# A fused perceiver layer on one core: two counted loops on the engines written out as straight code

## The chip, the core and the metric

The kernel runs on one core of a Trainium2 chip. It has five instruction streams: TensorE (PE, whose weight loads the profile shows apart as PEld), VectorE (DVE), ScalarE (ACT), GpSimd (POOL) and SyncE (SP, which here only issues DMAs). Each works through its own program, and they meet only at semaphores. The metric is device time in microseconds; lower is better.

## What is computed

64 sequences of 32 tokens, 256 features each, in float32 (2048 tokens). The reference, cut to what matters:

```python
def layer(x, ctx_1024, ...):
    # 1: cross attention over 257 context rows per sequence, keys through a cosine
    K_hat = cos((ctx @ Wk + bk) @ Wr + br)
    x = x + softmax((layernorm(x) @ Wq + bq) @ K_hat.T) @ (ctx @ Wv + bv)
    # 2: self attention over the 8 most similar earlier tokens, then a gated gelu
    h = layernorm(x); A = causal_topk(h @ h.T / 16, 8)
    msg = softmax(where(A, (h @ Wq2.T) @ (h @ Wk2.T).T / sqrt(32), -1e9)) @ h
    x = x + gelu((mix * h + (1 - mix) * msg) * gain + bias) * scale
    # 3: mixture of 8 experts, one per token
    e = argmax(layernorm(x) @ Wr); p = max(softmax(layernorm(x) @ Wr))
    return x + p * (gelu(layernorm(x) @ W1[e] + b1[e]) @ W2[e] + b2[e])
```

## The kernel before

**Groups and steps.** The 2048 tokens are 16 groups (`NG`) of 128. A function `step` exists on PE, DVE, ACT and POOL; step s works on group s in stage 0 (`now`: transposing the context rows, projecting them, the cosine), on group s-1 in stage 1 (`one`: softmax and weighted sum), s-2 in stage 2 (`two`: similarities, the 8 best), s-3 in stage 3 (`three`) and s-4 in stage 4 (`four`: gelu, router). So there are 21 steps, s = 0 to 20, and from step 4 to step 15 all five stages are at work. From step 7 on, odd steps also do the ranks of the router for a pair of groups (`rank`, `places`, `scatter`). The order of instructions on each engine is written out by hand in `step`, and semaphore waits stand before the instructions that need them.

**Expert blocks.** Tokens sorted by expert are run in 23 blocks (`NBLK`) of 128 rows. Each block gathers its rows (`gather`, POOL L445), transposes them (`in_T`, PE L1255 into pK), multiplies by the expert's W1 (`up`, PE L1334: 32 matmuls), takes the gelu (ACT L1154), multiplies by W2 (`down`, PE L1348: 16 matmuls), adds and stores (`result`, DVE L862, `store`, POOL L451). Blocks 0 to 6 (`EARLY` = 7) are mixed into steps 16 to 20 and a short straight piece behind them. Blocks 7 to 22 are `late_block`s.

**What is a loop.** `run_steps` writes steps 0 to 5 out (`PEELED` = 6), then runs a counted loop on each engine of two turns of four steps (steps 6 to 9 and 10 to 13), then writes steps 14 to 20 out. SP has a loop of its own over the same groups (L593). `run_late` runs blocks 7 to 18 as a loop of three turns of four blocks on PE, DVE and ACT and writes blocks 19 to 22 out; POOL and SP have the late blocks written out already. In a loop the group number is a register, so the count that a semaphore has to reach is a register too:

```python
def at_least(eng, sem, count):
    if not isinstance(count, int) or count > 0:
        eng.wait_ge(sem, count)

def settle(eng, sem):
    eng.wait_ge(sem, 1)

def in_register(eng, count):
    return count if isinstance(count, int) else eng.to_reg(count)
```

`settle` is a wait that is always met, placed ahead of waits on registers.

**The names in the rows.** `stage` holds context rows, their transposes and the cosine's inputs and outputs; `pT` and `pK` are the PSUM banks of the context transposes and projections, and of the expert blocks later. The first DVE instruction of a step is the copy `stage<-pT` (L739, `ctx_T_copy`), the first on PE are eight transposes into `pT` (L1255), then two of `xn`, then the scores (L1407).

Of the kernel before, what the change touches and what calls it, by code (L numbers as in the profile page):

```python
# [45 lines left out]
PEELED = 6  # L46

def at_least(eng, sem, count):

    if not isinstance(count, int) or count > 0:
# [12 lines left out]

def upto(value, most):

    return min(value, most) if isinstance(value, int) else value

def groups(k, parity, behind):

    g = 2 * k + parity - behind
    if isinstance(g, int) and not 0 <= g < NG:
        return None
    return g, (parity - behind) % 2, k + (parity - behind) // 2

def pair(k, kp):  # L80

    q = k - 3
    if isinstance(q, int) and not 0 <= q < NG // 2:
        return None
    return q, 2 * ((kp + 1) % 2)

def run_steps(eng, step):

    for s in range(PEELED):  # L90
        step(s // 2, s % 2, s // 4, s // 2 % 2)
    with eng.Fori(0, (NG - 2 - PEELED) // 4) as i:
        for k, half, kp in ((3 + 2 * i, 1 + i, 1), (4 + 2 * i, 2 + i, 0)):
            step(k, 0, half, kp)
            step(k, 1, half, kp)
    for s in range(NG - 2, NG + STAGES):
        step(s // 2, s % 2, s // 4, s // 2 % 2)

def run_late(eng, block):  # L100

    turns = WAVES[-1][1] // SLOTS
    with eng.Fori(0, turns - 1) as k:
        for q in range(SLOTS):
            block(EARLY + SLOTS * k + q, (EARLY + q) % SLOTS, k + (EARLY + q) // SLOTS)
    for q in range(SLOTS):
        j = EARLY + SLOTS * (turns - 1) + q
        block(j, j % SLOTS, j // SLOTS)

def following(j, q, turn):
    return j + 1, (q + 1) % SLOTS, turn + (q + 1) // SLOTS

def perceiver_layer(nc, a, out):
    ctx = ExitStack()
    with ctx:
# [221 lines left out]
        def _(pool):  # L339
# [72 lines left out]
            def scatter(q, r0, turn):  # L412

                s = r0 // 2
                count = in_register(pool, 16 + 32 * turn)
                settle(pool, S["consts"])
                pool.wait_ge(tokens_st[s], count)
                pool.tensor_copy(token_now[:, r0:r0 + 2], token_all[:, bass.ds(2 * q, 2)]).then_inc(S["token_r"], 1)
                count = in_register(pool, q + 1)
                settle(pool, S["consts"])  # L420
# [7 lines left out]
            def count_pair(q):  # L428
                count = in_register(pool, q + 1)
                settle(pool, S["consts"])  # L430
                pool.wait_ge(S["onehot_r"], count)
                pool.tensor_copy(so_far[:, 0, :], so_far[:, 2, :]).then_inc(S["count_r"], 1)
                settle(pool, S["consts"])
# [21 lines left out]
            def step(k, parity, half, kp):  # L455
                now, one, two, three, four, coming = (groups(k, parity, n) for n in (0, 1, 2, 3, 4, -1))
                routed, s = pair(k, kp), 2 * k + parity if isinstance(k, int) else None
# [4 lines left out]
                if now:  # L462
                    g, b, _ = now
                    if isinstance(g, int) and g == 0:
                        pool.wait_ge(S["khat_last_r"], 1)

                    settle(pool, S["consts"])
# [7 lines left out]
                if two:  # L475
                    g, b, _ = two
                    count = in_register(pool, g - 1)
                    settle(pool, S["consts"])
# [4 lines left out]
                if one:  # L483
                    g, b, q = one

                    counts = [in_register(pool, n) for n in (g + 1, 16 * BG * (q + 1))]
                    settle(pool, S["consts"])
# [39 lines left out]
            run_steps(pool, step)  # L527
# [11 lines left out]
        def _(sp):  # L539
# [49 lines left out]
            for g in range(2, PEELED):  # L589
# [986 lines left out]
```

## Time and profile before

| | |
|---|---|
| median of 3 timed runs | 520.58 us (519.25, 520.58, 527.82) |
| the profiled execution, its own time | 522.69 us |
| its span (first to last instruction) | 520.6 us |
| PE busy / DVE busy / ACT busy / POOL busy | 456.7 / 286.1 / 268.8 / 186.8 us |
| mean granted TensorE clock | 0.948 of full speed |

The span is what the trace covers; 2.1 us of the profiled execution lie around it. "Busy" counts only instructions that an engine's datapath executes. Waits, register arithmetic, branches and the issue of DMAs don't count.

### The profile page before, as it was taken

The numbers are of one execution on the slowest core, as the hardware profiler recorded it, in microseconds if no ns is written. First come the engines' busy times: TensorE is split into PE (matmuls) and PEld (weight loads), VectorE is DVE, ScalarE is ACT, GpSimd is POOL, SyncE is SP. The second block draws the span as 40 slices with busy tenths as digits, with TensorE's granted clock in tenths as the row PEclk, the third lists the DMA queues.
The fourth block names the chain that finished last, engine by engine and source line by source line (L and its number), as shares of the span: only waits on it lengthen the run. The fifth ranks groups of instructions, "written<-read, shape, count | busy, mean of one in ns | idle before, by whom it ended". The sixth has DMA issues, their size and how long they took to land. (4 is left out here: it accounts for less than half of the span.)

```text
span 520.6 us, 10379 instructions
## 1 busy us (share of the span) xinstructions
PE 456.7 (88%) x2839; PEld 336.9 (65%) x2840; DVE 286.1 (55%) x904; ACT 268.8 (52%) x587; POOL 186.8 (36%) x326
## 2 busy tenths in 40 slices
PE   4889999999999759999999167985977999999992
PEld 3545565666666426666665055885967899999992
DVE  1556778888898548898898334763321121222220
ACT  2366768877788527788777233534213132233320
POOL 2732235334653414653545043442231332223210
PEclk9799999999999969999999768899999899999997
DMA  8612522325415305415551090353549556555300
GB/s 229 206 39 93 171 92 64 110 93 173 132 44 171 91 1 171 132 43 170 171 174 42 0 362 22 99 207 118 146 124 373 150 203 212 206 178 171 125 0 1
DMA packets 49106, 69.13 MB, mean 133 GB/s; under 512 B 8702, under 2 KB 38976, under 8 KB 48932
## 3 DMA queue, kind: packets, MB, share of 16 engines
q1 hardware_dynamic: 42820, 59.12, 34.6%
q0 software_dynamic: 3520, 8.23, 4.6%
q10 hardware_dynamic: 2720, 1.26, 0.9%
q8 instruction: 18, 0.29, 0.2%
q14 instruction: 28, 0.23, 0.2%
HBM read 62.20 MB, written 7.30 MB: 133 GB/s over the span
## 5 line engine op out<-in xcount | busy, mean ns | idle before, releaser
L1311 PE MATMUL pK<-stage,Wkr 128*128 128x512 f32 x256 | 126.2, 619 | 9.8 <-DVE stage L739 9.2
L1154 ACT ACTIVATE XF<-pT,b_now 128x128 f32<-128x128 f32 x184 | 52.6, 368 | 119.3 <-PE pT L1334 82.3
L1334 PE MATMUL pT<-XF,stage 128*128 128x128 f32 x736 | 92.0, 285 | 4.5 <-DMA stage<-in_L_ffn_W_dram 4.5
L1334 PEld LDWEIGHTS pT<-XF,stage 128*128 128x128 f32 x736 | 90.9, 201 | 6.9 <-issue 5.8
L1348 PE MATMUL pK<-W,XF 128*128 x368 | 87.0, 387 | 2.9 <-issue 1.3
L1348 PEld LDWEIGHTS pK<-W,XF 128*128 128x128 f32 x368 | 68.7, 193 | 12.6 <-issue 3.9
L1311 PEld LDWEIGHTS pK<-stage,Wkr 128*128 128x128 f32 x256 | 45.3, 196 | 48.7 <-issue 48.2
L356 POOL TENSOR_SCALAR ve<-mv 128x1 f32<-128x1 f32 x48 | 13.3, 276 | 157.2 <-DVE mv L662 157.1
L1135 ACT ACTIVATE stage<-pK,bkr 128x512 f32<-128x512 f32 x64 | 42.9, 689 | 34.5 <-PE pK L1311 33.0
L1142 ACT ACTIVATE stage<-stage 128x512 f32<-128x512 f32 x64 | 40.5, 633 | 20.4 <-DVE stage L734 20.2
L734 DVE TENSOR_TENSOR stage<-stage 128x512 f32<-128x512 f32 x64 | 47.7, 746 | 1.2
L445 POOL DMA_INDIRECT f_row<-rows_by_token,token_i x23 | 22.7, 987 | 71.1 <-DMA out_dram<-XF,token_i 37.7
L451 POOL DMA_INDIRECT out_dram<-XF,token_i x23 | 23.4, 1017 | 65.1 <-DVE XF L862 62.8
L1255 PE MATMUL pT<-ident,stage 128*128 128x128 f32 x260 | 36.4, 284 | 7.3 <-DMA br<-in_L_xattn_br_dram 6.5
L855 DVE COPY XF<-pK 128x256 f32<-128x256 f32 x23 | 9.8, 424 | 57.1 <-PE pK L1255 56.1
L728 DVE TENSOR_SCALAR stage<-stage 128x512 f32<-128x512 f32 x64 | 29.3, 458 | 17.1 <-ACT stage L1135 14.8
L862 DVE SCALAR_TENSOR_TENSOR XF<-pK,f_row 128x256 f32<-128x256 f32 x23 | 11.1, 484 | 47.7 <-PE pK L1348 45.4
L1255 PEld LDWEIGHTS pT<-ident,stage 128*128 128x128 f32 x260 | 30.1, 148 | 10.8 <-issue 10.5
L358 POOL TENSOR_TENSOR rs<-ve,minus_half 128x1 f32<-128x1 f32 x48 | 34.4, 716 | 4.0
L739 DVE COPY stage<-pT 128x512 f32<-128x512 f32 x32 | 21.8, 681 | 10.1 <-issue 10.0
L425 POOL DMA_INDIRECT tokens_by_expert<-token_now,place x16 | 17.8, 1110 | 18.5 <-DVE place L782 11.6
L1407 PE MATMUL b<-stage,qT 128*32 128x257 f32 x256 | 17.2, 386 | 4.4 <-ACT stage L1142 4.4
(194 smaller groups left out, 696.2 us busy)
## 6 DMA issues: line engine op xcount, KB each, us to landing
stage<-in_L_ffn_W_dram SPq DMA_DIRECT2D x23, 1024.0 KB
stage<-in_ctx_dram SPq DMA_DIRECT2D x32, 512.0 KB, 4.9
W<-in_L_ffn_W_dram SPq DMA_DIRECT2D x8, 1024.0 KB, 5.9
rows_by_token<-rows_out SPq DMA_DIRECT2D x16, 256.5 KB
ctx_last<-in_ctx_dram SPq DMA_DIRECT2D x64, 32.0 KB, 4.0
X<-in_x_dram SPq DMA_DIRECT2D x1, 1792.0 KB, 7.5
stage<-in_L_ffn_b_dram SPq DMA_DIRECT2D x1, 1024.0 KB, 9.0
token_i<-tokens_by_expert SPq DMA_DIRECT2D x23, 0.5 KB
```

Source lines behind the costliest of these rows:

```text
L358: pool.tensor_tensor(rs[:], ve[:], minus_half[:], ALU.pow).then_inc(S[rs_r], 1)
L445: pool.indirect_dma_start(f_row[:, j % SLOTS, :], None, rows, bass.IndirectOffsetOnAxis(ap=token_i[:, j:j + 1], axis=0)).then_inc(f_row_ld ...
L451: pool.indirect_dma_start(out_v, bass.IndirectOffsetOnAxis(ap=token_i[:, j:j + 1], axis=0), f_out[:, j % 2, :], None, bounds_check=TOK - 1 ...
L728: v.tensor_scalar(frac[b], turns[b], ROUND, ROUND, ALU.add, ALU.subtract).then_inc(S["whole_r"], 1)
L734: v.tensor_tensor(frac[b], turns[b], frac[b], ALU.subtract).then_inc(S["frac_r"], 1)
L1135: act.activation(turns[r], pK[r][:], ACT.Identity, bias=bkr[:, r:r + 1]).then_inc(S["turns_r"], 1)
L1142: act.activation(khat[b][:, r, 2 * half:2 * half + 2, 0:CF], frac[r].rearrange("p (j n) -> p j n", j=2), ACT.Sin, scale=TWO_PI).then_inc(S ...
L1154: ins = act.activation(f_hT[b][:, n * P:(n + 1) * P], pT[i][:, (n % 4) * P:(n % 4 + 1) * P], ACT.Gelu, bias=b1_now[:, b, n:n + 1])
L1255: ins = pe.transpose(dst, src, ident[0:k, 0:k])
L1311: mm = pe.matmul(pK[r][:], Wkr[:, c, r * P:(r + 1) * P], ctx_T[:, c, half * 512:(half + 1) * 512], start=c == 0, stop=c == DC - 1)
L1334: mm = pe.matmul(pT[i][:, (n % 4) * P:(n % 4 + 1) * P], W1[q][:, c, n * P:(n + 1) * P], f_inT[:, q % 2, c * P:(c + 1) * P], start=c == 0, ...
L1348: mm = pe.matmul(p_out, f_hT[q % 2][:, n * P:(n + 1) * P], W2[:, bass.ds(e, 1), n, :].rearrange("p o d -> p (o d)"), start=n == 0, stop=n ...
```

## The change

All counted loops go. `run_steps` calls `step` for s = 0 to 20 with plain numbers, the late blocks are a Python loop, and SP's loads are written out as well. Every semaphore count is then a constant. `settle`, `in_register`, `upto`, `following` and `run_late` go, and so do the register instructions behind them. Nothing is moved within a step, with one exception: SP used to issue the W2 load of expert 6 between the loads of groups 14 and 15 and that of expert 7 after them; now expert 7's comes first.

```diff
-def settle(eng, sem):
-    eng.wait_ge(sem, 1)
-def in_register(eng, count):
-    return count if isinstance(count, int) else eng.to_reg(count)
...
-def run_steps(eng, step):
-    for s in range(PEELED):
+def run_steps(step):
+    for s in range(NG + STAGES):
         step(s // 2, s % 2, s // 4, s // 2 % 2)
-    with eng.Fori(0, (NG - 2 - PEELED) // 4) as i:
-        for k, half, kp in ((3 + 2 * i, 1 + i, 1), (4 + 2 * i, 2 + i, 0)):
-            step(k, 0, half, kp)
-            step(k, 1, half, kp)
-    for s in range(NG - 2, NG + STAGES):
-        step(s // 2, s % 2, s // 4, s // 2 % 2)
-def run_late(eng, block):
-    turns = WAVES[-1][1] // SLOTS
-    with eng.Fori(0, turns - 1) as k:
-        for q in range(SLOTS):
-            block(EARLY + SLOTS * k + q, (EARLY + q) % SLOTS, k + (EARLY + q) // SLOTS)
-    for q in range(SLOTS):
-        j = EARLY + SLOTS * (turns - 1) + q
-        block(j, j % SLOTS, j // SLOTS)
...
@@ POOL, rstd (the same pattern in scatter, count_pair, step, and on DVE)
-                count = in_register(pool, g + 1)
-                settle(pool, S["consts"])
+                count = g + 1
                 pool.wait_ge(S[mv_r], count)
...
@@ SP
-            for g in range(2, PEELED):
+            for g in range(2, NG):
                 next_group(g, g % 2)
                 if g % 2:
                     load_w2(g // 2 - 1)
-            with sp.Fori(0, (NG - 2 - PEELED) // 4) as i:
-                for k, r0 in ((3 + 2 * i, 0), (4 + 2 * i, 2)):
-                    next_group(2 * k, 0)
-                    next_group(2 * k + 1, 1)
-                    load_w2(k - 1)
-                    keep(k - 3, r0)
-            next_group(NG - 2, 0)
-            load_w2(NG // 2 - 2)
-            next_group(NG - 1, 1)
-            load_w2(NG // 2 - 1)
-            keep(4, 0)
+                if g % 2 and g >= 7:
+                    keep((g - 7) // 2, (g - 7) % 4)
+                if g == NG - 2:
+                    load_w2(NG // 2 - 1)
...
@@ PE (DVE and ACT alike)
-            run_late(pe, late_block)
+            for j in range(EARLY, NBLK):
+                late_block(*ring(j))
```

What this does to an engine's program, where the loop of the steps ends. Line numbers of the changed kernel are lower by about 55. On DVE before, the last instructions of step 9 (and of step 13), the loop's end, and what stands behind it, which is step 14:

```order
L734 TENSOR_TENSOR stage<-stage 128x512 [waits whole_r]
L1054 TENSOR_TENSOR y_msg<-b,gain_msg 128x256 [waits msg_mm]
L1060 ISA [waits xb_r,aproj]
L1060 TENSOR_TENSOR X<-b,X 128x256
L1070 COPY logits<-b 128x8 [waits route_mm]
L92 REGISTER_ALU
L92 COMPARE_AND_BRANCH
L739 COPY stage<-pT 128x512 [waits kproj,ctxT_tr]
L655 BN_STATS st<-X 128x6 [waits rs2_r,x1_r,consts]
L890 COPY xnT<-b 128x256 [waits qproj,xnT_tr]
```

The branch goes back to the head of the loop, which on DVE stands in the program as follows, behind the end of step 5:

```order
L1060 TENSOR_TENSOR X<-b,X 128x256 [waits xb_r,aproj]
L1070 COPY logits<-b 128x8 [waits route_mm]
L92 UNCONDITIONAL_BRANCH
L92 ISA
L52 REGISTER_ALU [waits ctxT_tr]
L739 COPY stage<-pT 128x512 [waits kproj]
L883 REGISTER_ALU [waits consts]
L52 REGISTER_ALU [waits x1_r]
L655 ISA [waits rs2_r]
L655 BN_STATS st<-X 128x6
```

On DVE in the changed kernel, the same place at the end of one of the steps that the loop held, and the start of the next:

```order
L679 TENSOR_TENSOR stage<-stage 128x512 [waits whole_r]
L991 TENSOR_TENSOR y_msg<-b,gain_msg 128x256 [waits msg_mm]
L997 TENSOR_TENSOR X<-b,X 128x256 [waits xb_r,aproj]
L1007 COPY logits<-b 128x8 [waits route_mm]
L684 COPY stage<-pT 128x512 [waits kproj,ctxT_tr]
L602 BN_STATS st<-X 128x6 [waits rs2_r,x1_r]
L831 COPY xnT<-b 128x256 [waits qproj,xnT_tr]
```

The branch and the register instructions are gone; the next step's copy stands right behind the copy of `logits`. DVE's program grows from 882 instructions to 1073. On PE before, the head of the loop:

```order
L1524 MATMUL b<-Wroute,xn3T 128x8
L92 UNCONDITIONAL_BRANCH
L92 ISA
L52 ISA [waits ctx_ld0]
L1255 MATMUL pT<-ident,stage 128x128 [waits ctxT0_cp]
L1255 MATMUL pT<-ident,stage 128x128 x3
L1255 MATMUL pT<-ident,stage 128x128 [waits ctxT1_cp]
L1255 MATMUL pT<-ident,stage 128x128 x3
L1392 REGISTER_ALU
L52 REGISTER_ALU [waits xn_r]
L52 REGISTER_ALU [waits selected]
L1255 MATMUL b<-ident,xn 128x128 [waits ymsg_r]
```

And in the changed kernel:

```order
L1463 MATMUL b<-Wroute,xn3T 128x8
L1194 MATMUL pT<-ident,stage 128x128 [waits ctxT0_cp,ctx_ld0]
L1194 MATMUL pT<-ident,stage 128x128 x3
L1194 MATMUL pT<-ident,stage 128x128 [waits ctxT1_cp]
L1194 MATMUL pT<-ident,stage 128x128 x3
L1194 MATMUL b<-ident,xn 128x128 [waits ymsg_r,selected,xn_r]
L1194 MATMUL b<-ident,xn 128x128
```

The matmuls stand in the same order, and the waits that sat on instructions of their own are now on the matmuls. The body of the steps' loop is 239 instructions on DVE, 131 on ACT and 93 on POOL; the body of the late blocks' loop is 68 on DVE and some 270 on PE. (These are counts of the listing, with one weight load for each matmul; the trace records each float32 matmul as two, so on PE its counts are larger.) In the same way of counting, PE's program grows from 2669 instructions to 3610, ACT's from 474 to 571, POOL's from 303 to 330; SP's shrinks from 366 to 360. The late blocks have one more pair of places. On DVE before, the end of the loop of late blocks:

```order
L848 SCALAR_TENSOR_TENSOR f_row<-stage,f_row 128x256
L52 ISA [waits f_y_mm,f_b2_r,consts]
L862 SCALAR_TENSOR_TENSOR XF<-pK,f_row 128x256 [waits f_y_st0]
L103 REGISTER_ALU
L103 COMPARE_AND_BRANCH
L829 TENSOR_LOAD expert_i
L829 ISA x2
L839 ISA [waits f_gelu]
L839 COPY b_now<-b_T 128x8
```

And the same kind of place between two late blocks in the changed kernel:

```order
L791 SCALAR_TENSOR_TENSOR f_row<-stage,f_row 128x256
L804 SCALAR_TENSOR_TENSOR XF<-pK,f_row 128x256 [waits f_y_st0,f_y_mm,f_b2_r]
L772 TENSOR_LOAD expert_i
L772 ISA x2
L782 ISA [waits f_gelu]
L782 COPY b_now<-b_T 128x8
```

The branch and one instruction that only waited are gone; reading the expert's number (`TENSOR_LOAD`) stays.

## Rows read from the trace of the kernel before

**Rows 1.** The page's head, and TensorE's granted clock in 40 slices (tenths)

```profile
span 520.6 us, 10379 instructions
...
PEclk9799999999999969999999768899999899999997
```

**Rows 2.** Busy time by stretch: us; PE, PEld, DVE, ACT, POOL; PEclk, DMA share, GB/s

```profile
100.00:120.00 20.00, 20.00 (x140) 12.61 (x138) 17.91 (x59) 16.21 (x30) 8.83 (x17) 1.00 0.19 60
...
180.00:200.00 20.00, 11.65 (x56) 6.58 (x57) 10.31 (x35) 7.16 (x13) 6.25 (x13) 0.74 0.03 3
```

**Rows 3.** Timeline of PE, 60 to 300 us: the transposes of xn, one pair per step

```profile
94.81 0.38 PE L1255 MATMUL b<-ident,xn 128*128 128x128 f32 x2
111.09 0.38 PE L1255 MATMUL b<-ident,xn 128*128 128x128 f32 x2
...
177.13 0.38 PE L1255 MATMUL b<-ident,xn 128*128 128x128 f32 x2
205.82 0.38 PE L1255 MATMUL b<-ident,xn 128*128 128x128 f32 x2
...
255.33 0.38 PE L1255 MATMUL b<-ident,xn 128*128 128x128 f32 x2
271.71 0.38 PE L1255 MATMUL b<-ident,xn 128*128 128x128 f32 x2
```

**Rows 4.** Timeline of DVE, 172 to 204 us: start, duration, operation, [idle before]

```profile
186.96 0.69 DVE L739 COPY stage<-pT 128x512 f32<-128x512 f32 x1 [9.64 <-issue]
...
189.56 0.43 DVE L655 BATCH_NORM_STATS2 st<-X 128x6 f32 x1 [1.90 <-issue]
```

**Rows 5.** Timeline of PE in the same stretch

```profile
177.49 1.07 PE L1407 MATMUL b<-stage,qT 128*32 128x257 f32 x16
...
187.79 3.78 PE L1311 MATMUL pK<-stage,Wkr 128*128 128x512 f32 x4 [9.22 <-DVE stage L739]
...
192.12 0.69 PE L1255 MATMUL b<-ident,h 128*128 128x128 f32 x2 [0.56 <-DVE h L667]
```

**Rows 6.** Timeline of ACT in the same stretch: its first instruction of step 10

```profile
177.41 0.59 ACT L1128 COPY stage<-pT 128x512 f32<-128x512 f32 x1 [0.16 <-PE pT L1255]
```

**Rows 7.** DMA queue of code: packets, MB, share; 177 to 178, 187 to 188, 189 to 190 us

```profile
q14 instruction: 1, 0.01, 12.7%
...
q14 instruction: 1, 0.01, 3.5%
...
q14 instruction: 1, 0.01, 3.0%
```

**Rows 8.** The same queues, 120 to 168 us

```profile
q8 instruction: 3, 0.05, 0.5%
q14 instruction: 5, 0.04, 0.4%
```

**Rows 9.** Waits of DVE, 120 to 176 us: total, times, longest

```profile
DVE stage L728 <- issue: 0.5, 1, 0.5
```

**Rows 10.** Late blocks: timeline of DVE, three copies of b_now

```profile
447.47 0.17 DVE L839 COPY b_now<-b_T 128x8 f32 x1 [0.47 <-issue]
...
455.08 0.21 DVE L839 COPY b_now<-b_T 128x8 f32 x1 [0.79 <-issue]
...
498.02 0.17 DVE L839 COPY b_now<-b_T 128x8 f32 x1 [0.30 <-issue]
```

**Rows 11.** Late blocks: timeline of PE, four of the L1334 rows

```profile
446.15 3.73 PE L1334 MATMUL pT<-XF,stage 128*128 128x128 f32 x32
...
453.40 3.73 PE L1334 MATMUL pT<-XF,stage 128*128 128x128 f32 x32
...
489.62 3.73 PE L1334 MATMUL pT<-XF,stage 128*128 128x128 f32 x32
...
496.87 3.73 PE L1334 MATMUL pT<-XF,stage 128*128 128x128 f32 x32
```

**Rows 12.** Steps 15 and 16: timeline of POOL and PE, 282 to 303 us

```profile
284.90 0.96 POOL L425 DMA_INDIRECT tokens_by_expert<-token_now,place  x1 [0.30 <-issue]
...
298.54 0.99 POOL L445 DMA_INDIRECT f_row<-rows_by_token,token_i  x1 [12.67 <-DMA token_i<-tokens_by_expert]
...
301.08 0.69 PE L1255 MATMUL b<-ident,h 128*128 128x128 f32 x2 [10.80 <-DVE h L667]
```

**Rows 13.** Blocks 7 and 9: timeline of PE, 380 to 405 us

```profile
389.28 3.83 PE L1334 MATMUL pT<-XF,stage 128*128 128x128 f32 x32 [2.34 <-DMA stage<-in_L_ffn_W_dram]
...
403.86 0.44 PE L1255 MATMUL pK<-ident,f_row 128*128 128x128 f32 x2 [2.09 <-DMA f_row<-rows_by_token,token_i]
```

More of the change, by code:

```diff
@@ L45 @@
 STAGES = 5
-PEELED = 6
 def at_least(eng, sem, count):
-    if not isinstance(count, int) or count > 0:
+    if count > 0:
         eng.wait_ge(sem, count)
-def settle(eng, sem):
-    eng.wait_ge(sem, 1)
-def in_register(eng, count):
-    return count if isinstance(count, int) else eng.to_reg(count)
-def upto(value, most):
-    return min(value, most) if isinstance(value, int) else value
 def groups(k, parity, behind):
     g = 2 * k + parity - behind
-    if isinstance(g, int) and not 0 <= g < NG:
+    if not 0 <= g < NG:
         return None
@@ L456, in step @@
                 now, one, two, three, four, coming = (groups(k, parity, n) for n in (0, 1, 2, 3, 4, -1))
[L457 removed]
+                routed, s = pair(k, kp), 2 * k + parity
                 if s in (17, 19):
@@ L463, in step @@
                     g, b, _ = now
-                    if isinstance(g, int) and g == 0:
+                    if g == 0:
                         pool.wait_ge(S["khat_last_r"], 1)
-                    settle(pool, S["consts"])
                     at_least(pool, S["scoresA"], g - 1)
@@ L670, in stats_x @@
             def stats_x(g):
-                if isinstance(g, int) and g in (0, 2):
+                if g in (0, 2):
                     v.wait_ge(S["x_ld" if g == 0 else "xrest_ld"], 16)
-                settle(v, S["consts"])
                 at_least(v, S["rs1_r"], g)
@@ L774, in places @@
                                 ).then_inc(S["inplace_r"], 1)
-                if isinstance(q, int) and 2 * q + 2 in [n for n, _ in WAVES]:
+                if 2 * q + 2 in [n for n, _ in WAVES]:
                     v.tensor_copy(count_e[:], p_count).then_inc(S["count_cp"], 1)
@@ L939, in step @@
                     end(1)
-                if routed and not parity and (s is None or s < 18):
+                if routed and not parity and s < 18:
                     route(routed[0])
@@ L1079, in step @@
                     plan_rows(3)
-            run_steps(v, step)
+            run_steps(step)
             def late_block(j, q, turn):
-                if not isinstance(j, int) or j + 1 < NBLK:
-                    bias1(*following(j, q, turn))
-                    in_T(*following(j, q, turn))
+                if j + 1 < NBLK:
+                    bias1(*ring(j + 1))
+                    in_T(*ring(j + 1))
                 bias2(j, q, turn)
@@ L1159, in step @@
                 now, one, two, three, four = (groups(k, parity, n) for n in (0, 1, 2, 3, 4))
-                routed, s = pair(k, kp), 2 * k + parity if isinstance(k, int) else None
+                routed, s = pair(k, kp), 2 * k + parity
                 if now:
@@ L1247, in _ @@
                 late_block(*ring(j))
-            run_late(act, late_block)
+            for j in range(EARLY, NBLK):
+                late_block(*ring(j))
         @block.tensor
@@ L1374, in step @@
                 now, one, two, three, four = (groups(k, parity, n) for n in (0, 1, 2, 3, 4))
-                routed, s = pair(k, kp), 2 * k + parity if isinstance(k, int) else None
+                routed, s = pair(k, kp), 2 * k + parity
                 r4 = (2 * kp + parity) % 4
@@ L1537, in late_block @@
                 up(j, q, turn, 1)
-                if not isinstance(j, int) or j + 1 < NBLK:
-                    in_T(*following(j, q, turn))
+                if j + 1 < NBLK:
+                    in_T(*ring(j + 1))
                 down(j, q, (0, 1))
@@ L1548, in _ @@
                 down(j, j % SLOTS, (1,))
-            run_late(pe, late_block)
+            for j in range(EARLY, NBLK):
+                late_block(*ring(j))
 _INS = ["x", "ctx_1024", "L0_xattn_Wq", "L0_xattn_bq", "L0_xattn_Wk", "L0_xattn_bk", "L0_xattn_Wv", "L0_xattn_bv",
```

74 lines of the change are left out of this document (28 added, 46 removed).

## The prediction

> **What bounds the kernel now.** I read the page first, then busy time by stretch, then the timeline of each engine where the stretches differ. The page gives a span of 520.6 us and, in the row of TensorE's clock, two dips behind the start: the digit 6 at 182 to 195 us (slices are 13 us long), and the digits 7688 at 286 to 338 us [rows 1]. Busy time by stretch says what a normal stretch is: between 100 and 120 us PE is busy for 20.00 of 20 us at full clock, with DVE at 17.91 [rows 2]. PE is the bound of the steps. Between 180 and 200 us it is busy for only 11.65 us at a mean clock of 0.74, and the DMA queues move 3 GB/s, so it isn't waiting for data [rows 2]. The reader should see in these two rows that one stall of some 10 us lies in the steps.
>
> To place it I took one instruction that occurs once per step on PE, the transposes of `xn` [rows 3]. Step 6 passes it at 111.09 us and step 10 at 177.13: four steps in 66.04 us, 16.51 each. Steps 11 to 14 take (255.33 - 205.82) / 3 = 16.50 each. Between step 10 and step 11 lie 28.69 us. That interval is 12.2 us too long, and it begins where the loop of steps jumps back, since step 10 is the first of its second turn.
>
> Who waits for whom there: PE ends its scores at 178.56 and stands until 187.79, idle 9.22 us by DVE's copy L739 [rows 5]. DVE's copy had been idle for 9.64 us by "issue", that is by nothing the profile shows, and the next DVE instruction stands idle for another 1.90 us in the same way [rows 4]. ACT, which waits for the same transposes as DVE's copy, starts its own at 177.41, 0.16 us after its last work [rows 6]. So the inputs of the copy were there. What DVE did in that time, PE and ACT didn't have to do, or did at once: all of them had jumped back.
>
> What it was is shown by the queue that carries code: one packet lies in 177 to 178 us, one in 187 to 188, one in 189 to 190, each where DVE begins or ends one of its two idle times [rows 7, 4]. The loop's body on DVE is 239 instructions, on ACT 131, on POOL 93; DVE's is the longest but for PE's. I take it that DVE's code for the head of the loop had to be read again after the jump. The Trainium skill says so too, in "Runtime: NRT & Kernel Launch", section on instruction fetch mechanics: code is prefetched in sequence only, and a taken branch to a block that isn't held has to wait for a DMA. It gives no price for that wait, and the rows are the only place for one.
>
> **The sum, part by part.** It is made against the profiled execution: 522.69 us, of which 520.6 is span.
>
> Term 1, the jump back of the steps' loop. It goes away on all engines at once. Step 10 to 11 shrinks from 28.69 to the 16.5 of its neighbours: 12.2 us. It is made of PE's 9.22 us of waiting; the slower clock behind it, where four matmuls of L1311 take 3.78 us [rows 5]; 0.56 us of waiting for `h` [rows 5], which is DVE's second idle time passed on; the rest is the remainder of the slow clock. What is late next: PE itself, fully busy before and after. Nothing else was hidden beneath the gap that could now come up, since a second engine reading code at that moment would have been reading it because of the same jump. Loads can't be late either: each group's context is loaded when a step finishes, so the loads move with the steps.
>
> Term 2, register arithmetic, `settle` and the two loop ends in the steps. Steps in the loop take 16.50 to 16.51 us. Of the two neighbours in straight code, step 5 takes 111.09 - 94.81 = 16.28 and step 14 takes 271.71 - 255.33 = 16.38 [rows 3]. Eight steps at the second difference are 8 x 0.12 = 1.0 us, at the first 8 x 0.23 = 1.8. But step 5 has no router work for a pair and step 14 is an even one, without the matmuls of `rank` that each odd step holds, so part of the difference is work and stays. The lower end is 0. I take half of the nearer, 0.5 us.
>
> Term 3, the late blocks' loop. DVE's gap before `b_now` is 0.47 us inside the loop, 0.79 where the loop jumps back, 0.30 in straight code [rows 10]. But PE is what bounds there: a block is 453.40 - 446.15 = 7.25 us long in the loop, across the time of that jump, and 496.87 - 489.62 = 7.25 us in straight code [rows 11]. PE has no idle time in either. The value is 0; PE's own work covers it, and without that cover it would be 12 x 0.17 + 2 x 0.3 = 2.6 us. That two jumps back cost DVE only 0.3 us each here is noted for a rival.
>
> Term 4, more code to be read. PE's program grows by 941 instructions and DVE's by 191. Straight code is read ahead: from 120 to 168 us, inside the first turn, eight packets of code were read [rows 8], and DVE's longest idle time by "issue" was 0.5 us [rows 9]. I take 0. The bounds are 0 and one stall like the one of term 1, 12.2 us, each time it isn't read ahead.
>
> Term 5, SP. The order of the last two W2 loads is swapped. Both must have landed before the first `down`, and both are issued within the same two steps. 0 either way.
>
> Behind the steps nothing changes order. At the start of the expert blocks POOL stands for 12.67 us until the first token list has been written out and read back, and PE stands for 10.80 us with it [rows 12]. That chain starts with `places` in step 15, so it moves as a whole and gives back nothing. The waits for W1 (2.34 us) and for gathered rows (2.09 us) in blocks 7 and 9 [rows 13] depend on the same chain of DMAs that POOL and SP issue from straight code already. They may come out a few microseconds different by chance; I take 0, with 3 us either way.
>
> Sum: 12.2 + 0.5 = 12.7 us. The profiled execution would take 522.69 - 12.7 = 510.0 us with a span of 507.9. The median of the runs lies 2.1 us under the profiled execution; I carry the saving over whole: 520.58 - 12.7 = **507.9 us**, a ratio of 0.976. About 2% is what a measurement of this kernel can tell from no change, so the forecast stands only just outside it: the border is at 510.2.
>
> **The rivals.**
> A. *The end of a block of code costs something in straight code too.* DVE's second idle time, 1.90 us, came at its second instruction after the jump, and with a packet of its own [rows 4, 7]. If that was the ordinary price of going on to the next block when reading ahead has just begun, some of it stays, and the gap may also be shorter in executions without a profiler. For it: the profiled execution is 2.1 us slower than the median. Against it: no such idle time in rows 9. Price: 1.9 us and the 0.56 us on PE stay, 2.5 us in all, for 510.4 us; two such places, 513.
>
> B. *The gap isn't the jump's.* Then straight code has it too, somewhere, and only term 2 is gained: 520.1 us. For it: the same kind of branch back cost DVE 0.3 us in the late loop [rows 10], and the late loop's body is only 68 instructions, so size may be the difference or may not. The Trainium skill has two rules on this side. "Advanced Engine Details and Errata", section on control flow timing, puts a compare-and-branch at about 108 ns; by it two loop ends are an estimated 0.2 us. And the page on the runtime has room for 512 instructions in two blocks on engines other than PE, by which DVE's 239 could be held whole and the jump would read nothing; rows 7 show packets at that moment, which speaks against it. Against it also: the seven intervals within the two turns and the two beside them have no such gap [rows 3], and the one that has it begins at the jump.
>
> C. *Slower: PE's code comes late in the late blocks.* Before, PE ran blocks 7 to 18 out of a loop of some 270 instructions that needed no new code after its first turn. Now it reads new code all the time, while W1 loads of 1 MB fill the same 16 engines. If a packet of code is late there, PE stands as DVE did. The price is that of term 1, 12.2 us each: one such stall takes back the gain (520.1), from two on it is slower, 532 us. For it: PE's program grows most. Against it: PE used 7.25 us per block in the straight blocks 19 to 22 as well [rows 11], and its code was read in time between 120 and 168 us, when it was fully busy.
>
> D. *More than forecast.* The waits of rows 13, 4.4 us together, are met in time because of a chance shift among the DMAs: 503.5 us.
>
> **How the numbers follow.** Forecast 0.64 (504.5 to 510.2: term 2 at either end, and the late waits by some 3 us down and 2 up). A 0.16 (510.2 to 513.5). B 0.09 (519 to 521). C 0.06 (520 and up, mostly 532). D 0.05 (501 to 504.5). Faster by over 2% is the forecast and D, less a little for the border: 0.66. Slower by over 2% is the larger part of C and what I haven't thought of: 0.06. The rest, 0.28, is within 2%. The range of 8 in 10 takes in the forecast, A, and the nearer part of D, and leaves out B and C: 503 to 515 us.
>
> **What the changed kernel's profile would show.** Term 1: the transposes of `xn` at even distances of 16.3 to 16.5 us from step 5 to step 15, DVE without an "issue" wait above 1 us there, and no dip of the clock before the expert blocks. Term 2: those distances near 16.4 instead of 16.5. Term 3: 7.25 us per late block as before. Term 4: more packets on the two code queues, spread evenly, and none with an idle engine beside it. Rival A would show as idle times of 1 to 2 us by "issue" on DVE at some packets. B would show a gap of about 9 us on one engine in one step. C would show PE idle by "issue" among the late blocks. The prediction is wrong if the gap turns up elsewhere, or if the start of the expert blocks takes longer than the 10.80 us that PE stands there now.

## The result and the profile after

The changed kernel takes 505.58 us (median of 4 runs, 504.69 to 507.41), the kernel before beside it on the same chip 522.17 us (519.25 to 527.82). The ratio is 0.9705, with a 95% interval of 0.9639 to 0.9771: faster. It is not the ratio of these two medians (0.968), since it leaves out the one execution of 527.82 us, which fell in a slower state of the chip. The forecast was a ratio of 0.976, 507.9 us. The profiled execution took 507.41 us with a span of 505.7, against 522.69 and 520.6: 15.3 us less, where 12.7 were forecast.

The page of the changed kernel, its head, the row of the clock and the two queues of code:

```profile
span 505.7 us, 9537 instructions
...
PEclk9999999999999999999999678998998999999997
...
q8 instruction: 24, 0.39, 0.4%
q14 instruction: 24, 0.20, 0.2%
```

The first dip of the clock in [rows 1] is gone. The second, before the expert blocks, stands at about the same place in the work.

TensorE's timeline after, the transposes of `xn` once per step (start, length, engine, line, operation); the row before the first "..." is step 5's, the next three are those of steps 9 to 11, the last one is step 15's:

```profile
97.40 0.38 PE L1194 MATMUL b<-ident,xn 128*128 128x128 f32 x2
...
162.63 0.38 PE L1194 MATMUL b<-ident,xn 128*128 128x128 f32 x2
178.97 0.38 PE L1194 MATMUL b<-ident,xn 128*128 128x128 f32 x2
195.26 0.38 PE L1194 MATMUL b<-ident,xn 128*128 128x128 f32 x2
...
260.51 0.38 PE L1194 MATMUL b<-ident,xn 128*128 128x128 f32 x2
```

All ten intervals lie between 16.29 and 16.34 us. Before, they were 16.28 to 16.61, and one of 28.69 ([rows 3] hold the ends of the stretches). DVE's waits between 100 and 275 us, which is the whole answer (us in total, times, longest):

```profile
DVE stage L673 <- ACT stage L1073: 7.8, 10, 0.8
DVE h L613 <- POOL rs L319: 5.9, 11, 0.5
DVE o_T L974 <- PE b L1194: 2.8, 6, 0.7
DVE xn L613 <- POOL rs L319: 2.6, 6, 1.0
```

None of them is by "issue" (the profile's word for idle time in which the engine waited for nothing that it shows), and TensorE has no wait at all in that stretch. Busy time by stretch, after, in the middle of the steps, and in the stretch behind the first transposes of `h` of the expert blocks, where the clock is slow (columns as in [rows 2]):

```profile
160.00:180.00 20.00, 20.00 (x143) 13.28 (x140) 16.88 (x53) 15.96 (x31) 9.51 (x15) 1.00 0.44 140
312.00:318.00 6.00, 6.00 (x39) 5.71 (x39) 5.33 (x23) 3.60 (x9) 1.58 (x3) 0.74 0.14 47
```

About the same work as the second row, before:

```profile
324.00:330.00 6.00, 6.00 (x30) 5.45 (x29) 4.82 (x21) 3.54 (x9) 1.48 (x3) 0.54 0.32 88
```

The last but two of the numbers is the granted clock: 0.74 of 2.4 GHz after, 0.54 before. So the execution before spent more of this stretch at the lower of TensorE's two clocks, 1.2 GHz, than the one after. That leads to an account of the 15.3 us by stretches of the two timelines:

| stretch | before, us | after, us | saved |
|---|---|---|---|
| start to `xn` of step 5 | 94.81 | 97.40 | -2.59 |
| `xn` of step 5 to that of step 15: the interval of step 10 | 28.69 | 16.29 | 12.40 |
| the same: the nine other intervals | 148.21 | 146.82 | 1.39 |
| step 15 to the first transposes of `h` behind POOL's wait | 29.37 | 29.38 | 0.0 |
| from there to the ranks of the last pair of groups | 62.46 | 59.81 | 2.65 |
| from there to the end | 157.06 | 156.0 | 1.1 |

The rows sum to the difference of the spans, 14.9 us; the rest of the 15.3 lies around them. The first row is the same code in both kernels, and over the fourteen kernels of the table below it scatters from 93.55 to 97.40 us. From step 15 to the end the kernel before took 248.9 us, the changed one 245.2, the twelve others of that table 247.0 to 252.1. Rows 2 and 3 are the ones that other kernels repeat.

### The profile page after: what moved, and what is told of

Same layout as the page of the kernel before. It is cut to its first block and busy times, and to the rows that moved or that the text cites. A ratio compares the mean times of both kernels' runs of the same rounds, so it can differ in the third digit from the quotient of the medians.

```text
span 505.7 us, 9537 instructions
## 1 busy us (share of the span) xinstructions
PE 452.9 (90%) x2839; PEld 336.4 (67%) x2839; DVE 283.6 (56%) x903; ACT 268.5 (53%) x587; POOL 188.8 (37%) x326
## 5 line engine op out<-in xcount | busy, mean ns | idle before, releaser
L1250 PE MATMUL pK<-stage,Wkr 128*128 128x512 f32 x256 | 123.6, 608 | 0.5 <-ACT stage L1066 0.4
L317 POOL TENSOR_SCALAR ve<-mv 128x1 f32<-128x1 f32 x48 | 15.2, 317 | 142.9 <-DVE mv L608 142.8
L673 DVE TENSOR_SCALAR stage<-stage 128x512 f32<-128x512 f32 x64 | 27.6, 430 | 17.5 <-ACT stage L1073 16.7
L319 POOL TENSOR_TENSOR rs<-ve,minus_half 128x1 f32<-128x1 f32 x48 | 35.7, 743 | 4.0
L384 POOL DMA_INDIRECT tokens_by_expert<-token_now,place x16 | 16.4, 1026 | 16.5 <-DVE place L725 10.1
```

Source lines behind the costliest of these rows:

```text
L319: pool.tensor_tensor(rs[:], ve[:], minus_half[:], ALU.pow).then_inc(S[rs_r], 1)
L673: v.tensor_scalar(frac[b], turns[b], ROUND, ROUND, ALU.add, ALU.subtract).then_inc(S["whole_r"], 1)
L1250: mm = pe.matmul(pK[r][:], Wkr[:, c, r * P:(r + 1) * P], ctx_T[:, c, half * 512:(half + 1) * 512], start=c == 0, stop=c == DC - 1)
```

## The experiments

All edits are made to the kernel before. Twelve kernels ran in three sets of four, each set on one chip with its own runs of the kernel before (medians 523.7, 523.7 and 523.3 us). Each expectation names its theories itself. Two measures carry most of the reading: the interval of step 10 (from the `xn` transposes of step 10 to those of step 11, 28.69 us in [rows 3]) and the largest of the other nine between steps 5 and 15.

| kernel | ratio (95% interval) | step 10, us | largest other | steps 5 to 15 |
|---|---|---|---|---|
| before | | 28.69 | 16.61 | 176.90 |
| after | 0.9705 (0.9639 to 0.9771) | 16.29 | 16.34 | 163.11 |
| DVE's steps straight | 0.9756 (0.9718 to 0.9793) | 16.47 | 16.52 | 164.23 |
| all but DVE's steps straight | 0.9988 (0.9953 to 1.0023) | 29.03 | 17.89 | 178.16 |
| PE's steps straight | 0.9976 (0.9944 to 1.0007) | 29.08 | 16.53 | 176.76 |
| hint on all four loops | 0.9911 (0.9873 to 0.9949) | 16.44 | 24.37 | 174.02 |
| hint on DVE's loop | 0.9874 (0.9831 to 0.9917) | 16.44 | 20.45 | 169.17 |
| late blocks straight | 0.9962 (0.9931 to 0.9993) | 28.27 | 16.72 | 176.77 |
| DVE's loop head at slot 0 | 0.987 (0.9788 to 0.9952) | 16.42 | 20.03 | 168.48 |
| at slot 64 | 1.011 (1.0029 to 1.0192) | 27.31 | 19.11 | 178.87 |
| at slot 128 | 0.9769 (0.9677 to 0.9861) | 16.42 | 17.00 | 164.91 |
| longer late loop on DVE | 0.9994 (0.9954 to 1.0033) | 30.74 | 17.03 | 179.89 |
| the same blocks straight on DVE | 0.9968 (0.9943 to 0.9993) | 28.89 | 17.11 | 177.50 |
| longer late loop, head at slot 64 | 1.0024 (0.9982 to 1.0066) | 28.67 | 17.04 | 177.46 |

**How long the loops are.** The counts of instructions given so far (239, 131, 68, 941 more) are those of a listing in which the waits on semaphores are folded into other instructions. The compiled programs hold most of them as instructions of their own, 64 bytes each like every other, and are longer:

| | before | after |
|---|---|---|
| PE, whole program | 4582 | 6322 |
| DVE, whole program | 1252 | 1460 |
| DVE, body of the steps' loop | 340 | |
| DVE, body of the late loop | 77 | |
| ACT / POOL, body of the steps' loop | 196 / 135 | |

The traffic on the queues of code bears these counts out, and not those of the listing. 4582 instructions are 0.29 MB and 6322 are 0.40 MB; the queue q8, whose packets are 16 KB, read 0.29 MB before and 0.39 MB after. The other queue, q14, has packets of 8 KB, which is 128 instructions; by the totals it serves the other four engines (in the kernel with slot 128 they have 2956 instructions, 0.19 MB, and it read 0.19 MB). The texts written before each run say 239 and 228 for two of DVE's loops; compiled, they are 340 and 238.

**Which engine's loop, 1: DVE's steps alone written out** (e1_dve_steps_straight). Late blocks, SP and the other three engines keep their loops.

```diff
+def straight_steps(step):
+    for s in range(NG + STAGES):
+        step(s // 2, s % 2, s // 4, s // 2 % 2)
...
@@ DVE
-            run_steps(v, step)
+            straight_steps(step)
```

> Only VectorE gets its steps written out; the other engines and all late blocks keep their loops. Theory 1 (VectorE reads the code at its loop's head again after the jump back): the interval between steps 10 and 11 falls from 28.7 to about 16.5 us, and the kernel is about 12 us faster than before (ratio 0.977), leaving 3 to 4 us to the changed kernel. Theory 2 (the jump costs because several engines, TensorE with them, read code again at once, or because of the loop's register waits): TensorE, ScalarE and GpSimd still jump back, so at least part of the gap stays, on another engine; ratio 0.985 to 1.0. Steps within the loop stay at 16.5 us if TensorE's own register instructions make them longer than 16.3, and fall to 16.3 if VectorE's do.

Measured: 510.64 us, ratio 0.9756. TensorE's timeline of this kernel, `xn` in steps 10 and 11:

```profile
178.31 0.38 PE L1261 MATMUL b<-ident,xn 128*128 128x128 f32 x2
194.78 0.38 PE L1261 MATMUL b<-ident,xn 128*128 128x128 f32 x2
```

16.47 us: the gap is gone, with PE, ACT and POOL still jumping back at this place.

**2: the mirror image** (e2_dve_steps_looped). `straight_steps(step)` on PE, ACT and POOL, `run_steps(v, step)` on DVE.

> The mirror of the first: TensorE, ScalarE and GpSimd get their steps written out, VectorE keeps its loop (SyncE and the late blocks too). Theory 1: VectorE's idle time of 9 to 10 us at the jump is there as before, the interval between steps 10 and 11 is 28 to 29 us, and the kernel is within 2 us of the one before. Theory 2: the gap is gone or is under 5 us, ratio 0.98 or lower.

Measured: 523.30 us, ratio 0.9988. DVE's timeline of this kernel at the end of step 9, the two rows that are idle by "issue" (idle time and releaser in brackets):

```profile
189.02 0.69 DVE L745 COPY stage<-pT 128x512 f32<-128x512 f32 x1 [10.10 <-issue]
...
191.41 0.43 DVE L661 BATCH_NORM_STATS2 st<-X 128x6 f32 x1 [1.70 <-issue]
```

The same two idle times as in [rows 4], 10.10 and 1.70 us. Step 8, from 144.52 us on, takes 17.89 us with 1.0 us of waiting by "issue" on PE, which stays unexplained. The gap is there with DVE's jump alone, and gone without it alone. It is DVE's.

**3: PE's steps alone written out** (e4_pe_steps_straight), the same edit on PE.

> Only TensorE gets its steps written out. Theory 1: the gap of 12.2 us stays, since VectorE still jumps. What this run shows beside it is the pace of the steps: if TensorE's register instructions and separate waits make the steps 16.5 us instead of 16.3, the pace falls to 16.3 and the kernel gains 1 to 2 us (ratio 0.997); if they don't, both stay.

Measured: 521.96 us, ratio 0.9976; 29.08 us for step 10, and PE waits 9.8 us for DVE's copy. The nine other intervals take 147.68 us, against 148.21 before and 146.82 after. The theory's gain of 1 to 2 us from PE's register instructions didn't come: the nine intervals give 0.5 us, and the interval of the ratio takes in 1. 847 more instructions in PE's compiled program (5429 against 4582) cost nothing that can be seen, which is most of term 4 by itself.

```diff
-    with eng.Fori(0, (NG - 2 - PEELED) // 4) as i:
+    with eng.bass.Fori(0, (NG - 2 - PEELED) // 4, engines=[eng.engine], hint_back_edge=True) as i:
```

 Theory 1: the gap shrinks to below 3 us without any code written out, ratio about 0.977, with the register instructions and steps of 16.5 us kept. If the gap is not a matter of reading code (theory 3: something in the second turn's data or semaphores), the hint changes nothing and the ratio is 1.0.

> The kernel before with the hint of a taken branch on VectorE's loop of steps alone. With the hint on all engines the gap at the jump back was gone (16.4 us from step 10 to 11), but 8 us came back in step 14, behind the loop's end, where TensorE, VectorE and ScalarE each stood without a reason that the profile shows. Theory 1a: each engine's hint makes it read the loop's head again at the last turn, where the branch is not taken, and so makes it wait for the code behind the loop. Then with the hint on VectorE alone only VectorE's part of that (an idle time of about 2.6 us) is left, and the kernel is 9 to 12 us faster than before, ratio 0.977 to 0.983. Rival: the loss behind the loop is VectorE's alone and comes whole; ratio 0.99 as with all hints.

Measured: 519.99 us, ratio 0.9911, with the hint on all four, and 516.08, ratio 0.9874, with the hint on DVE. In both the interval of step 10 is 16.44 us, so the loop's jump costs nothing. But of the 12.25 us won there, 8.0 or 4.1 us are lost in a new place, behind the loop's end, where step 14 takes 24.37 us with four hints and 20.45 with DVE's alone, instead of 16.38 [rows 3]. Timeline of the kernel with four hints, one row each of PE, DVE and ACT at that place:

```profile
254.00 0.92 PE L1255 MATMUL pT<-ident,stage 128*128 128x128 f32 x7 [2.38 <-issue]
254.93 0.69 DVE L734 TENSOR_TENSOR stage<-stage 128x512 f32<-128x512 f32 x1 [2.63 <-issue]
...
266.51 0.69 ACT L1135 ACTIVATE stage<-pK,bkr 128x512 f32<-128x512 f32 x1 [3.42 <-issue]
```

PE, DVE and ACT each stand for 2.4 to 3.4 us, and they don't stand at the same time; the three together are 8.4 us, about what step 14 lost. With four hints, step 12 also takes 17.66 us, which stays unexplained. No packet of code was read from 153 to 248 us, and the first one on q14 behind that comes within 0.7 us after DVE has stopped at 252.30 us and takes 1.4 us, so DVE seems to wait for it. With DVE's alone, DVE's row of the same instruction is:

```profile
254.42 0.69 DVE L734 TENSOR_TENSOR stage<-stage 128x512 f32<-128x512 f32 x1 [2.56 <-issue]
```

The price moves from the jump to the exit. The first expectation left that out, so its ratio of 0.977 failed. The second named it (theory 1a), and DVE does stand alone there, for 2.56 us as it said; but step 14 lost 4.1 us, the ratio lies outside the 0.977 to 0.983 that it gave, and its rival's 0.99 is inside the interval.

**6: the late blocks alone written out** (e6_late_straight).

```diff
@@ DVE, ACT, PE
-            run_late(v, late_block)
+            for j in range(EARLY, NBLK):
+                late_block(*ring(j))
```

> The kernel before with the late blocks written out on TensorE, VectorE and ScalarE, the loop of steps kept. Theory 1: nothing to gain, since TensorE bounds the late blocks at 7.25 us in the loop and in straight code; the time is within 1 us of before (ratio 0.998 to 1.002) and the gap at step 10 is there. Rival: the changed kernel's shorter stretch behind step 15 (245.2 us against 248.9) comes from the late loop's removal; then this one gains 2 to 4 us, ratio 0.993 to 0.996.

Measured: 521.01 us, ratio 0.9962 (0.9931 to 0.9993). A late block is 7.25 us long, as in [rows 11]. The ratio lies between what theory 1 allowed (0.998 and up) and what the rival asked (0.996 and down). Its interval is a gain of 0.4 to 3.6 us. In the profiled execution the stretch behind step 15 takes 247.1 us, 1.8 less than before, but kernels whose late blocks are unchanged also show 247.0 and 247.5 us there. So whether writing out the late blocks wins a microsecond or two stays open.

**7 and 8: is it the length of the loop?** In the late loop DVE's jump cost 0.3 us ([rows 10]), with a body of 77 compiled instructions, against 340 in the steps. 40 copies of one column into a tile that nobody reads are added to each late block on DVE, which makes the body 238 instructions (228 in the listing); once with the late loop (e7_dve_late_long_loop), once with DVE's late blocks written out (e8_dve_late_long_straight).

```diff
+            def small(n0):
+                for i in range(n0, n0 + 20):
+                    v.tensor_copy(junk[:, i:i + 1], minus_half[:])
             def late_block(j, q, turn):
+                small(0)
...
+                small(20 + 20 * (q % 2))
                 result(j, q, turn)
```

> The kernel before with 40 copies of one column more per late block on VectorE, which make the body of the late blocks' loop there 228 instructions instead of 68, nearly as long as that of the steps' loop (239). They write a tile that nobody reads. VectorE has 5 us to spare per late block and the copies take about 3. Theory 1 (a jump back over more code than the engine holds costs a reading): at the two jumps VectorE stands idle by 8 to 12 us each without a reason shown, and TensorE behind it, so this kernel is 12 to 20 us slower than its twin with VectorE's late blocks written out. Theory 4 (the cost belongs to the loop of steps, whatever its length): no such idle time, both twins alike.

> The twin: the same 40 copies, but VectorE's late blocks written out one behind the other (832 instructions more in its program than before), TensorE's and ScalarE's still in their loop, the steps' loop kept. Both theories: no idle time of VectorE above 1 us without a reason shown among the late blocks, 7.2 to 8 us per block, and a time that is at most 10 us above the kernel before (what the copies themselves cost).

Measured: 523.23 us, ratio 0.9994, and 522.20, ratio 0.9968 (0.9943 to 0.9993). The expectation of a gap at the late jumps failed. DVE's waits by "issue" in the kernel with the long late loop, from 400 to 500 us:

```profile
DVE f_row L849 <- issue: 6.4, 14, 0.8
DVE b_now L840 <- issue: 2.7, 11, 0.3
```

The longest is 0.8 us, and PE needs 7.245 us per block. By the listing the two loops, 228 and 239, looked alike in length, and the next expectations take from it that length doesn't decide. Compiled they are 238 and 340, so this pair doesn't test that; the next three kernels do. In the steps, which it doesn't touch, the first of the two takes 30.74 us for step 10, where the other kernels with a stall there take 27.31 to 29.08; that stays unexplained.

**9, 10 and 11: is it where the loop lies?** Three kernels in which DVE's loop of steps keeps its code and its length, and only its place in the program is set. Slot n puts the head at instruction n of a stretch of 256; the slots in front are filled and the entry jumps over them (e9_slot0, e10_slot64, e11_slot128).

```diff
-    with eng.Fori(0, (NG - 2 - PEELED) // 4) as i:
+    with eng.bass.Fori(0, (NG - 2 - PEELED) // 4, engines=[eng.engine], head_slot=slot) as i:
...
-            run_steps(v, step)
+            run_steps(v, step, slot={v.engine: 128})
```

> The kernel before, with VectorE's loop of steps placed in its program so that the loop's first instruction stands at the start of a block of code. Nothing else changes. The long late loop showed that 228 instructions can be jumped back over for nothing, so length alone doesn't decide. Theory 1c: the code is held in blocks of 128 instructions (8 KB, the size of the packets on that queue), and the jump costs when the body touches three of them. From slot 0 the body of 239 touches two: no gap, 16.4 us from step 10 to 11, ratio about 0.977. Theory 1d: a length near 239 is too long wherever it stands: the gap of 12 us stays.

> As the last, with the loop's first instruction at slot 64 of a block of 256. The body of 239 then touches three blocks of 128, and two of 256. Theory 1c: the gap of 12 us is there, as before, ratio 1.0. If blocks are of 256, this one behaves like slot 128.

> As the last, at slot 128. The body touches two blocks of 128, and two of 256. Theory 1c: no gap, ratio 0.977, as at slot 0. Blocks of 256 with one held: the gap is there, as at slot 64.

Measured: 515.15 us (0.987), 527.94 us (1.011) and 511.17 us (0.9769); forecast by theory 1c were 0.977, 1.0 and 0.977. DVE's copy behind the jump back, in the kernel with slot 64, and in the one with slot 128:

```profile
187.02 0.69 DVE L739 COPY stage<-pT 128x512 f32<-128x512 f32 x1 [8.50 <-issue]
```

```profile
177.17 0.68 DVE L739 COPY stage<-pT 128x512 f32<-128x512 f32 x1
```

At slots 0 and 128 the jump costs nothing (16.42 us for step 10), at slot 64 it costs 8.50 us of waiting (27.31 us). Between 170 and 249 us q14 reads 5 packets in the kernel before and 5 at slot 64, and none at slots 0 and 128. The loop's length is the same in all of them, so length alone doesn't decide. The kernels with slots 0 and 64 pay where the entry jumps over the filling: DVE stands for 2.41 and 2.62 us, and step 6 takes 20.03 and 19.11 us. In the kernel with slot 0:

```profile
113.87 0.69 DVE L739 COPY stage<-pT 128x512 f32<-128x512 f32 x1 [2.41 <-issue]
```

At slot 128 that isn't seen (16.61 us). So placement alone wins what writing out DVE's steps wins: 0.9769 against 0.9756. A packet on q14 is 8 KB (0.20 MB in 24). By the Trainium skill, "Runtime: NRT & Kernel Launch", section on instruction fetch mechanics, 16 KiB are 256 instructions, so 8 KB are an estimated 128. The compiled body of 340 touches three stretches of 128 from slot 0 or 128, and four from slot 64. Where it lay before it touches four too, if the program itself starts at the start of a stretch (the head is its instruction 317). The recorded expectations have one less in each case, since they reckon with 239. By the page's own rule, two blocks of 256 held, the body touches two blocks from every slot, so all three slots should behave alike; the 8.50 us at slot 64 alone speak against it, and the measurement decides.

**12: the late loop across three stretches** (e12_late_long_slot64): the long late loop of 7, DVE's head at slot 64.

```diff
-            run_late(v, late_block)
+            run_late(v, late_block, slot={v.engine: 64})
```

> The kernel with 40 more copies per late block on VectorE, in its late loop (228 instructions), which showed no idle time at its jumps, now with that loop's head at slot 64. Its body touches three blocks of 128 there. Theory 1c: VectorE stands idle at the two jumps, by up to 9 us each, of which 2 to 5 us are covered by its spare time, so TensorE waits for 4 to 7 us twice and the kernel is 8 to 14 us slower than the same without the placement. If no jump there costs anything, it is not the number of blocks but something of the steps' loop alone.

Measured: 523.31 us, ratio 1.0024 (0.9982 to 1.0066). DVE's waits by "issue" in this kernel from 400 to 500 us:

```profile
DVE f_row L849 <- issue: 5.3, 13, 0.5
DVE b_now L840 <- issue: 2.7, 11, 0.3
```

No jump stalls, and the forecast of 8 to 14 us failed. But the forecast rested on the listing's count. A compiled body of 238 instructions from slot 64 touches three stretches of 128, as many as the steps' loop touches from slots 0 and 128, where it doesn't stall either. All loops on DVE side by side:

| loop on DVE | instructions, compiled | stretches of 128 touched | wait at the jump back |
|---|---|---|---|
| steps, as before | 340 | 4 (if as said above) | 9.64 us |
| steps, slot 64 | 340 | 4 | 8.50 us |
| steps, slots 0 and 128 | 340 | 3 | none |
| late | 77 | 2 | 0.3 us |
| late, longer | 238 | 3 | none |
| late, longer, slot 64 | 238 | 3 | none |

So one account fits every row: DVE has room for four stretches of 128, and one of them is taken by the code that it reads ahead. A body of three stays, and so does the code behind it; a body of four pushes out its own head. The hint fits as well: it keeps the read-ahead from the code behind the loop, so four stretches stay (no code read from 153 to 248 us), and the first stretch behind the loop is missing at the exit. At slot 128 nothing was read on q14 for as long, from 162 to 251 us, and DVE has no wait by "issue" at the exit. This account was put together after all runs, from rows of these runs; no run was made to try it.

## Why the prediction was right

**Term 1, the jump back of the steps' loop: right, in cause and size.** 12.2 us were taken, 12.4 measured (28.69 to 16.29). That it is DVE's own, and not another engine's, was argued from [rows 4 to 6] and is now shown by the pair 1 and 2: its code written out alone gives 0.9756, all other engines' code written out 0.9988. That what it waits for is code is supported more strongly than before: with the instructions of the loop unchanged, a hint or another place in the program makes the 9.6 and 1.9 us vanish, and the packets of code with them. One premise was off: it gave DVE's body as 239 instructions, and compiled it is 340. The argument from rows doesn't use that number. The rule that the prediction cited from the Trainium skill, that a taken branch to code that isn't held waits for it, agrees with that.

**Term 2, registers and loop ends: the one term that was mis-sized.** 0.5 us were taken, within 0 to 1.8; measured are 1.4 us in the nine other intervals, where all now take 16.29 to 16.34 us. The step that was off is the halving: the prediction put part of the difference between steps in the loop and in straight code down to the ranks of the router in odd steps. From step 7 on, the odd steps after are only 0.01 to 0.05 us longer than the even ones, so nearly all of it went with the loop (register instructions, waits of their own and the loop's end; which of these isn't shown). With DVE's steps alone written out the nine take 147.76 us, with PE's alone 147.68: about 0.5 us each. Neither gives the 1.4 by itself.

**Term 3, late loops: 0 taken.** PE's late blocks are 7.245 us in both kernels. DVE's copy of `b_now` has only this in front of it now:

```profile
454.06 0.17 DVE L782 COPY b_now<-b_T 128x8 f32 x1 [0.28 <-issue]
```

As forecast this is hidden by PE. The interval of kernel 6 allows for a gain of 0.4 to 3.6 us from the late blocks, which the length of a block doesn't show.

**Term 4, more code: 0, right.** The growth was larger than the term said, compiled 1740 instructions on PE and 208 on DVE. q8 read 24 packets against 18, q14 24 against 28, since the five read again after the jump are gone. PE, DVE and ACT have no wait by "issue" between 100 and 275 us. **Term 5**, the W2 loads' order, has no trial of its own. The chain at the start of the expert blocks moved as a whole: POOL waits 12.87 us for the token list and PE 10.79, against 12.67 and 10.80 [rows 12]. The timeline after:

```profile
287.34 0.99 POOL L402 DMA_INDIRECT f_row<-rows_by_token,token_i  x1 [12.87 <-DMA token_i<-tokens_by_expert]
289.89 0.69 PE L1194 MATMUL b<-ident,h 128*128 128x128 f32 x2 [10.79 <-DVE h L613]
...
381.74 0.44 PE L1194 MATMUL pK<-ident,f_row 128*128 128x128 f32 x2 [3.63 <-DMA f_row<-rows_by_token,token_i]
```

The wait in the last row is that of block 9, 2.09 us in [rows 13], and the one of block 7, 2.34 us there, is now 1.41 us, by "issue" instead of the load of W1 (whether it is late code or the load isn't shown): 5.0 us for the two against 4.4. They did move by chance, inside the 3 us allowed.

**The rest of the difference.** The sum was 12.7 us, and the profiled executions differ by 15.3. Terms 1 and 2 measured are 13.8 us. The remaining 1.5 us is the balance of 2.6 us lost in the start, 3.7 us won behind step 15, 2.65 of them where TensorE's clock is slow, and 0.4 around the span. That these come from the change isn't shown. In the twelve experiments of the table that last stretch scatters from 247.0 to 252.1 us, by more than 3.7 us; but the changed kernel's 245.2 lies below all of them, so chance isn't shown either.

**The rivals.** A, an end of a block of code costs something in straight code as well: refuted in its place, no wait by "issue" on DVE in the steps. It returned elsewhere, 2.4 to 3.4 us where an engine leaves a hinted loop or jumps over filled slots. B, the gap isn't the jump's: refuted by kernels 1 and 2. The late loop that spoke for it does jump back without a stall, and its size is the likely difference, as B itself allowed. C, PE's code late in the late blocks: not seen, 7.245 us each. D, more than forecast: it didn't come. 505.58 us lies in the forecast's own range of 504.5 to 510.2, above D's, and the waits of rows 13, which D named, grew from 4.4 to 5.0 us. The forecast of 507.9 was still 2.3 us too high; the paragraph above says where the difference lies.

**Still open.** First, what DVE waits for between the end of its first packet of code, which takes 2.0 us from 177.5 us on [rows 7], and 186.96 us, when it goes on: no row shows it, and 7 us are long for reading 8 KB. The second and third packet begin only about when DVE goes on. Second, whether four stretches of which one is read ahead is the rule: a longer late loop of four stretches, or the steps' loop cut to at most 320 instructions at slot 64, would try it.

## What to carry to other kernels

Look in the timeline for one interval longer than its neighbours where a loop turns, and for an engine that is idle there by "issue" together with packets on its queue of code; then write out, or place, that engine's loop alone before touching the others. Here DVE's loop of 340 instructions carried 2.4 of the 2.95%, and setting the place of its head won the same as writing it out; the same edit at another slot lost 1.1%, so a placement is measured before it is kept. Count a loop in the compiled program, with its semaphore instructions: the listing's 239 instead of 340 is what led experiment 12 astray. The exit of a hinted loop cost 2.4 to 3.4 us per engine in these runs, and the jump over filled slots 2.4 and 2.6 us in two of three; engines that pay one after the other add up.

## What was not expected of the hardware

A jump back cost 9.6 and 1.9 us on DVE, with packets that take 2.0, 0.6 and 0.5 us. The place of a loop's head decided between 0 and 8.5 us with the same instructions. A hinted loop of two turns read no code for 95 us, and then PE, DVE and ACT stood for 2.4 to 3.4 us each in the code behind it; with the loop at slot 128 and no hint, q14 read nothing for 89 us, and DVE stood nowhere. A loop of 238 compiled instructions on the same engine, at two placements, paid nothing for its jumps.
